# A hand-written schedule, re-dealt: side jobs, gate steps, denominators and queue order of a two-layer recurrent block on one core

## What is computed

```python
xn = layernorm(x)
# s: differential attention, 8 heads of 32 features, two maps per head with 16 features each
scores = einsum('bqhif,bkhif->ibhqk', q, k) * 16 ** -0.5
att = softmax(scores)[0] - 0.2 * softmax(scores)[1]
o = einsum('bhqk,bkhe->bqhe', att, v)
s = ((o * rsqrt(mean(o * o) + eps) * norm_w) @ Wo.T + bo) * (1 - 0.2)
# g: per token the two best of 8 experts, softmax of their two logits, low-rank product
gate = sum(one_hot(top2) * softmax(top2 values))
g = silu(2.0 * einsum('btr,bte,eor->bto', xn @ compress.T, gate, routed))
x = x + s * g
```

## Time and profile before

| what | value |
|---|---|
| median of three runs | 1316.97 us (1316.34, 1316.97, 1319.7) |
| the profiled execution | 1319.7 us, of which the span is 1317.9 us |
| layer 0 (to the last exponential) | up to about 650 us of the span |
| PE, PEld | 1215.7 us (92%), 755.9 us (57%) |
| DVE, ACT, POOL | 954.9 us (72%), 675.7 us (51%), 594.1 us (45%) |
| mean granted clock of TensorE | 0.969 |

### The profile page before, as it was taken

One profiled execution on the slowest core, in us unless ns is written; L12 is line 12 of the kernel. 1 busy time (PEld: TensorE's weight loads), 2 busy tenths in 40 slices (PEclk: granted clock), 3 DMA queues, 4 the chain that ended last, 5 costly groups with the idle time before them and its releaser, 6 DMA issues. The chain is left out here.

```text
span 1317.9 us, 27919 instructions
## 1 busy us (share of the span) xinstructions
PE 1215.7 (92%) x10768; PEld 755.9 (57%) x10768; DVE 954.9 (72%) x2088; ACT 675.7 (51%) x1297; POOL 594.1 (45%) x613
## 2 busy tenths in 40 slices
PE   5899999999999999998859999998989999898997
PEld 4433443444434444443347786877768777786875
DVE  5776787877778787866346859676786967768675
ACT  2455656666666666665624434444444434434442
POOL 2156586766768676766533222131321213223131
PEclk9598999999999999999969999999999999999999
DMA  6644354454535354470220010100101000010100
GB/s 193 137 88 99 87 122 97 106 137 88 132 72 122 86 116 98 106 191 26 63 86 2 2 49 2 49 3 1 49 2 48 3 26 25 2 49 2 32 3 17
DMA packets 57972, 86.36 MB, mean 66 GB/s; under 512 B 8304, under 2 KB 38256, under 8 KB 57840
## 3 DMA queue, kind: packets, MB, share of 16 engines
q1 hardware_dynamic: 57840, 84.58, 26.7%
HBM read 50.40 MB, written 33.55 MB: 64 GB/s over the span
## 5 line engine op out<-in xcount | busy, mean ns | idle before, releaser
L975 DVE TENSOR_REDUCE negmax<-s_bank 128x1 f32<-128x512 f32 x512 | 331.4, 678 | 53.3 <-PE s_bank L669 52.8
L1139 POOL TENSOR_TENSOR room<-room 128x512 f32<-128x512 f32 x248 | 309.2, 1279 | 105.5 <-ACT room L816 105.5
L816 ACT ACTIVATE room<-t_bank 128x512 f32<-128x512 f32 x512 | 286.6, 599 | 76.0 <-PE t_bank L679 73.9
L669 PE MATMUL s_bank<-kst,qst 48*128 48x512 f32 x512 | 217.0, 491 | 13.5 <-DVE negmax L975 9.2
L679 PE MATMUL t_bank<-qst,kst 50*128 50x512 f32 x512 | 200.3, 466 | 12.2 <-ACT room L816 9.9
L679 PEld LDWEIGHTS t_bank<-qst,kst 50*128 50x128 f32 x512 | 81.3, 188 | 126.4 <-ACT room L816 75.6
L1857 POOL TENSOR_TENSOR win<-rt,apart 128x512 f32<-128x512 f32 x32 | 42.0, 1332 | 231.5 <-DVE rt L1682 231.5
L692 PE MATMUL a_bank<-room,v 128*32 128x512 f32 x1024 | 139.0, 615 | 0.0
L1844 POOL TENSOR_TENSOR ex<-ex,rc 128x256 f32<-128x256 f32 x64 | 41.9, 655 | 189.0 <-DVE rc L1710 189.0
L1725 DVE STREAM_TRANSPOSE room<-ex 32x256 f32<-32x256 f32 x256 | 111.1, 434 | 10.1 <-POOL ex L1844 4.1
L669 PEld LDWEIGHTS s_bank<-kst,qst 48*128 48x128 f32 x512 | 86.1, 193 | 37.1 <-DVE negmax L975 29.6
(11 more groups left out here) (258 smaller groups left out, 2274.5 us busy)
## 6 DMA issues: line engine op xcount, KB each, us to landing
park<-qk_h SPq DMA_DIRECT2D x128, 128.0 KB, 2.4
qst<-park SPq DMA_DIRECT2D x64, 192.0 KB, 3.6
kst<-park SPq DMA_DIRECT2D x64, 192.0 KB, 4.3
park<-qk_l SPq DMA_DIRECT2D x64, 128.0 KB, 2.4
room<-in_x SPq DMA_DIRECT2D x8, 512.0 KB, 5.7
xr<-in_x SPq DMA_DIRECT2D x8, 512.0 KB, 6.2
room<-x SPq DMA_DIRECT2D x8, 512.0 KB, 4.2
out<-so SPq DMA_DIRECT2D x32, 128.0 KB, 1.7
```

The lines of the kernel that those rows point to most:

```text
L669: pe.matmul(s_bank[S_BANK[w]][:, :], qst[slot][rows, j, c * P:(c + 1) * P], kst[slot][rows, j, :], start=True, stop=True).then_inc(m.s_don ...
L816: act.activation(probs[:, c, j, :], t_bank[w % 2][:, :], ACT.Exp, scale=SCALE0).then_inc(m.exp_done, 1)
L975: dve.tensor_reduce(negmax[:, i_par, 2 * odd + j, c:c + 1], s_bank[S_BANK[w]][:, :], X, ALU.max, negate=True).then_inc(m.max_done, 1)
L1139: add = pool.tensor_tensor(sums[:, pair, h, :], probs[:, 2 * pair, h, :], probs[:, 2 * pair + 1, h, :], ALU.add)
```

## The change

The tables of the schedule are dealt anew, and two orders are edited. No operation is added or removed.

- Side jobs change steps (`SLOTS`, `JOBS`): the second XT goes before the first V of the quarter; PROJ of quarter 4 goes from (1, 9) to (1, 3); PROJ 5 from (2, 1) to (2, 3); TA 2 and 3 from (1, 3) and (1, 5) to (1, 5) and (1, 7); the M jobs from w = 7 to w = 9; WF 1 and 2 from (2, 9) and (2, 13) to (2, 11) and (2, 14); V 0 of the next batch goes before PROJ 7.
- Denominators go from w = 1 and 7 to w = 3 and 7, where each stands behind a value step; the value bank's copy from w = 8 to 9; the denominators' copy from (0, 11) to (0, 10).
- Gate steps, normalisation and squares change steps.
- In SyncE's order `place_max` of quarter 1 goes ahead of `load_x`, `load_residual` and the weights; `place_max` of quarters 2 and 3 goes behind a park and a fill each; the stores are spread.
- In GpSimd's order `add_parts` goes ahead of `add_maps`, the first residual behind `add_pair(2, 0)`, the second behind `rstd_of`.

```diff
-SLOTS = ((0, 1), (0, 3), (0, 5), (0, 7), (0, 9), (0, 13), (0, 15),
+SLOTS = ((0, 1), (0, 3), (0, 5), (0, 9), (0, 11), (0, 13), (0, 15),
          (1, 1), (1, 3), (1, 5), (1, 7), (1, 9), (1, 11), (1, 13), (1, 15),
-         (2, 1), (2, 5), (2, 7), (2, 9), (2, 13),
-         (3, 1), (3, 5), (3, 7), (3, 9), (3, 13), (3, 15))
-JOBS = (("XT", 1, 0), ("V", 0, 2), ("XT", 1, 1), ("M", 1, 1), ("V", 0, 3), ("TD", -1, 0), ("TA", -1, 0),
-        ("TA", -1, 1), ("TA", -1, 2), ("TA", -1, 3), ("M", 2, 0), ("PROJ", 4, 0), ("ZT", -1, 0), ("OT", -1, 0), ("OT", -1, 1),
+         (2, 3), (2, 5), (2, 9), (2, 11), (2, 14),
+         (3, 1), (3, 5), (3, 9), (3, 11), (3, 13), (3, 15))
+JOBS = (("XT", 1, 0), ("XT", 1, 1), ("V", 0, 2), ("M", 1, 1), ("V", 0, 3), ("TD", -1, 0), ("TA", -1, 0),
+        ("TA", -1, 1), ("PROJ", 4, 0), ("TA", -1, 2), ("TA", -1, 3), ("M", 2, 0), ("ZT", -1, 0), ("OT", -1, 0), ("OT", -1, 1),
         ("PROJ", 5, 0), ("WF", -1, 0), ("M", 3, 1), ("WF", -1, 1), ("WF", -1, 2),
-        ("PROJ", 6, 0), ("WF", -1, 3), ("M", 4, 0), ("PROJ", 7, 0), ("V", 1, 0), ("V", 1, 1))
+        ("PROJ", 6, 0), ("WF", -1, 3), ("M", 4, 0), ("V", 1, 0), ("PROJ", 7, 0), ("V", 1, 1))
...
-STATS, NORM_ENDS, NORMS = ((2, 11), (2, 12)), (2, 14), ((3, 10), (3, 11), (3, 12), (3, 14))
-GATE = ((1, 7), (1, 8), (1, 11), (1, 12), (1, 13), (1, 14), (1, 15), (2, 3), (2, 4), (2, 7), (2, 8), (2, 10),
-        (2, 15), (3, 0), (3, 2), (3, 3), (3, 4), (3, 6))
-GATE_EXP = (2, 13)
-SQUARES = ((1, 11), (1, 12), (1, 14), (2, 0))
-SUM_STEPS, EVAC_STEP, DEVAC = (1, 7), 8, (0, 11)
+STATS, NORM_ENDS, NORMS = ((2, 11), (2, 12)), (2, 13), ((3, 10), (3, 12), (3, 14), (3, 15))
+GATE = ((1, 5), (1, 6), (1, 7), (1, 13), (1, 14), (1, 15), (2, 5), (2, 6), (2, 7), (2, 13), (2, 14), (2, 15),
+        (3, 1), (3, 2), (3, 3), (3, 4), (3, 5), (3, 6))
+GATE_EXP = (3, 0)
+SQUARES = ((1, 11), (1, 12), (1, 13), (1, 14))
+SUM_STEPS, EVAC_STEP, DEVAC = (3, 7), 9, (0, 10)
```

SyncE's order in `body(b)`:

```diff
+                place_max(i + 1, 1)
                 if b < B - 2:
                     load_x(b + 2)
                 if b:
                     load_residual(b - 1)
                 if last:
                     shared.load_weights(sp, io1)
-                place_max(i + 1, 1)
-                place_max(i + 2, 2)
-                if not last:
-                    park_parts(i + 4)
-                    fill_stacks(i + 4, 0)
-                    park_parts(i + 5)
-                    fill_stacks(i + 5, 1)
-                place_max(i + 3, 3)
-                for t in range(2):
-                    if b:
-                        store_x1(b - 1, t)
+                for hf in (1, 2):
+                    if not last:
+                        park_parts(i + 3 + hf)
+                        fill_stacks(i + 3 + hf, hf - 1)
+                    place_max(i + hf + 1, hf + 1)
+                if b:
+                    store_x1(b - 1, 0)
                 if not last:
                     park_parts(i + 6)
                     fill_stacks(i + 6, 2)
                 if b:
+                    store_x1(b - 1, 1)
+                if not last:
+                    place_max(i + 4, 0)
+                if b:
                     store_x1(b - 1, 2)
```

GpSimd's order in `body(b)`:

```diff
                 add_pair(b, 0, 1)
+                if not last:
+                    add_parts(b + 1)
                 if not first:
                     add_maps(b - 1)
...
                 add_pair(b, 1, 1)
+                add_pair(b, 2, 0)
                 if not first:
                     residual(b - 1, 0)
-                add_pair(b, 2, 0)
-                if not first:
-                    residual(b - 1, 1)
-                if not last:
-                    add_parts(b + 1)
                 add_pair(b, 2, 1)
                 if b < B - 2:
                     rstd_of(b + 2)
                 if not first:
+                    residual(b - 1, 1)
                     residual(b - 1, 2)
```

More of the change, by code:

```diff
@@ L569, in body @@
                 if b:
+                    store_x1(b - 1, 1)
+                if not last:
+                    place_max(i + 4, 0)
+                if b:
                     store_x1(b - 1, 2)
                 if not last:
-                    place_max(i + 4, 0)
                     park_parts(i + 7)
```

## The result

The changed kernel takes 1334.63 us (median of four runs, 1329.73 to 1339.92), against 1317.55 us for the kernel before in runs beside it. The ratio is 1.0129, with a 95% interval of 1.0082 to 1.0176: slower by 1.3%. The forecast was 1323.0, its range ended at 1332, and slower was its likeliest sign. So the sign is right, and the size lies outside the range. The profiled execution of the changed kernel took 1343.76 us, with a span of 1341.8; its counterpart of before 1319.7 and 1317.9.

The account below looks back on a forecast made before the run. TensorE was taken to set the pace, busy 72.9 of 75.0 us a batch. Steady batches +7.2, batch 0 +3 and batch 7 -4 gave +6.2 us on the median 1316.97, so 1323, range 1308 to 1332.

Parts of the forecast that it names:

- likeliest sign: Whole kernel: slower by over 0.3% had chance 0.52, within 0.3% 0.25, faster 0.23.
- rule (a): After XT or PROJ, misc frees 1.50 us later; two bare steps leave 0.75 us idle, three times a batch: 2.25 us.
- bare steps (2, 1) and (2, 2): Start of quarter 2, left without denominators and PROJ: (2, 2) waits for the exponential of (2, 0), 0.7 us a batch.
- Gate step 7: At (2, 6) VectorE arrives after GpSimd's pair starts and waits 1.1 us; the tile of (2, 11) then waits 0.7.
- Batch 0: First batch: stack wait and slow clock go (-7.8 us); two 2.5 us waits for maxima's rows, slow clock 6: +3.
- batch 7: Last batch: wait for maxima behind weights, its slow clock and a wait for GpSimd's sums go: -4 us.
- Net: 2.4 + 1.4 + 0.7 + 1.3 - 4.6 = +1.2 us a batch, x 6 = +7.2: Steady batches 1 to 6: job waits, M alone, bare steps and quarter 2, less VectorE's backlog and small savings.
- much slower: Rival: maxima's rows come after TensorE at every (2, 0), clock perhaps falling; +14 us, 1337; chance 0.12.
- M alone at w = 9: Steps 8 to 10: fourth tile held by exponentials, 0.38 us a quarter, 0.25 in quarter 1; 1.4 a batch.
- VectorE's backlog: Steady batch: excess at (3, 1), (3, 5), (1, 7) and other steps goes or is replaced, 3.5 us a batch.
- faster: Rival: in batch 0 place_max rows of quarters 2 and 3 pass the fill and land in time; 1307; chance 0.23.
- no change: Rival: VectorE comes first at (2, 6), or batch 0's waits don't slow the clock; 1317 to 1319; chance 0.25.

Follow-up runs that it names:

- experiment 3: Changed kernel with only gate steps 6 to 8 moved earlier, to (2, 3), (2, 4) and (2, 5): 1329.84 us, ratio 1.0080 to the kernel before.
- experiment 5: Changed kernel run again with nothing edited: 1339.67 us, ratio 1.0151 to the kernel before.
- experiment 6: Changed kernel with place_max of quarters 2 and 3 ahead of the fill, still behind the park: 1331.42 us, ratio 1.0092 to the kernel before.
- experiment 2: Changed kernel with only PROJ 5 moved back from (2, 3) to (2, 1): 1322.72 us, ratio 1.0028 to the kernel before.
- experiment 10: Changed kernel with the denominators back at w = 1 and 7: 1335.28 us, ratio 1.0127 to the kernel before.
- experiment 1: Changed kernel with four jobs re-dealt: V (0, 3), XT (0, 5), PROJ 4 (1, 1), TA 1 (1, 3), PROJ 5 (2, 1): 1315.41 us, ratio 0.9967.
- experiment 7: Kernel before with only the denominators moved, from w = 1 and 7 to 3 and 7: 1308.56 us, ratio 0.9924.

## Why the prediction was right and wrong

**Right: the mechanisms.** Each of the three job waits stands where it was put, 0.74 to 0.75 us, six times, by rule (a). The bare steps (2, 1) and (2, 2) cost 0.71 (said 0.7). Gate step 7 met GpSimd and took 1.17 us (said 1.1), and its whole term, removed in experiment 3, is 0.56 of the 0.7 given to the wait at (2, 11). Quarter 3 is 1.8 shorter (said 1.5). Batch 0 has the two waits behind the fill and the slow clock behind them, batch 7 has neither of its waits. The differences by quarter at full clock are +0.95, +1.24, +1.60 and -1.80; said were +0.5, +0.55, +1.45 and -1.5.

On gate step 7 the prediction could not settle who comes first; the trace does. GpSimd started at 337.36, VectorE at 337.52, 0.16 us later, for 1.17 us; in experiment 3, ahead of GpSimd, the same operation takes 0.18. By "SBUF — State Buffer", section "SBUF: two separate sides", of the Trainium skill, whichever of the two starts first holds the shared port pair for its whole instruction. The trace agrees: the later starter waited out the add.

**The step that failed** is "Net: 2.4 + 1.4 + 0.7 + 1.3 - 4.6 = +1.2 us a batch, x 6 = +7.2", and it failed twice.

First, it has no term for the granted clock. I priced the steady batch at 1.00 throughout, because the earlier trace rows show 1.00 in each quarter and I took both falls of before for the work of single waits of 1.64 and 1.87 us. In the changed kernel no wait in a steady batch exceeds 0.75 us, and the clock still fell at (2, 11), for 1.63 us each time: 8.2 us in the profiled execution, 3.3 and 4.9 in experiments 5 and 6. The trace of before already spoke against my reading. The stretch of 18.1 us at 0.63 in the earlier trace rows, which I put behind the wait of 1.64 us, is three in the main: 3.3 us at half clock behind the wait, 3.4 us at full clock, and 10.2 us at half clock behind two waits for exponentials of 0.44 and 0.56 us.

```profile
95.40:98.70 3.30, 3.30 (x19) 0.59 (x16) 1.38 (x3) 0.60 (x1) 1.92 (x2) 0.50 0.68 158
98.70:102.10 3.40, 2.40 (x21) 0.82 (x17) 2.34 (x4) 2.42 (x5) 3.40 (x4) 1.00 0.52 111
102.10:112.30 10.20, 9.94 (x40) 2.84 (x39) 7.96 (x20) 3.95 (x8) 6.88 (x5) 0.50 0.38 69
...
100.54 0.49 PE L679 MATMUL t_bank<-qst,kst 50*128 50x512 f32 x1 [0.44 <-ACT room L816]
...
101.61 0.50 PE L679 MATMUL t_bank<-qst,kst 50*128 50x512 f32 x1 [0.56 <-ACT room L816]
```

The rival "much slower" did have a falling clock, but tied to rows of maxima that come late at (2, 0); the rows were in time in every steady batch, and the clock fell without them. Removing the idle of (2, 1) to (2, 5) (experiment 2) or the gate's wait (experiment 3) ended the falls in quarter 2 in the profiled executions of both. That supports the idle of this quarter as their cause, but these are single profiles, falls moved to quarter 1 in experiment 2, and in experiment 10, where (2, 1) and (2, 2) are covered and the wait at (2, 5) is not, quarter 2 of batch 3 still lost clock.

Second, the terms at full clock were undersized by 0.8 in batches 1 to 5. By the timeline, M alone at w = 9 costs 2.1 us a batch, not 1.4 (0.62, 0.54, 0.37 and 0.54 by quarter, each step against the shortest of equal content), just past its bound of 2.0: steps 9 to 11 of quarter 0 take 0.83 + 0.49 + 2.71 us. What I left out is that the value matmuls of w = 11 also need the value bank, whose copy now sits at w = 9; their weight load waits 0.3 to 0.4 us for it. No run moved M alone; the nearest check is quarter 0 of experiments 1 and 7, which differ there in M, the V behind it and two copies on ScalarE: 17.36 against 16.86, 0.5 of the 0.62. And VectorE's backlog at (1, 7), counted as gone, stayed: 0.31 us there. In batch 6 the cost is 3.1, because that batch of before, 73.91 us, had less backlog to lose, and I took all six as alike. The bounds were added up wrongly as well: those of the four terms less 4.6 come to -2.8 and +3.7 a batch, and the text has -1.0 and +3.0.

By the profiled executions, then, said +6.2, measured +24.0. The missing 17.8 us are: clock in batches 2 to 6, 8.2; steady terms, 5.9 (13.1 less 7.2); batch 0, 1.9; batch 7, 1.5; unassigned, 0.3. The medians differ by 17.1 us, 10.9 more than said, and 9.3 of that would be the steady terms and the two outer batches, if they are alike in every execution. So the falls are the largest item of the longest execution. What they leave room for at the median, 1.6 us, is one fall; how many it had is not on record.

**Batch 0** was +4.9 instead of +3. The two waits were of 1.1 us each on TensorE (2.0 for its weight loads), not 2.5, and the 6.8 us at half clock behind each cost half of their busy time, 3.3 us, where I took 3. What I left out is the rest: the stretch of 3.4 us at 82 us, 1.7 us by the same estimate, and the job waits and bare steps of a steady batch, which stand in batch 0 too. Experiment 6, without any wait for rows, still has a batch 0 of 74.0 us, where before less the 7.8 us of its wait and clock would have 68.6. That experiment gets 7.2 us back against the first profile and 9.0 against experiment 5, whose batch 0 also began with more slow clock; experiment 1 gets 9.5 back with the jobs alone. One move in the queue is also what the rival "faster" needed: two small rows not behind the fill.

**Batch 7** was -2.5 instead of -4; its wait for the rows and the one for GpSimd's sums both went. I had counted the bare steps' loss of about 0.5 us once. Experiment 10 shows what the move of the denominators costs there: 2.3 us, 0.6 to 0.9 in three of the four quarters, which is more than the 1.5 missing.

**The rival "no change"** rested on VectorE coming first at (2, 6). Experiment 3 makes that so, and the kernel is still 0.8% slower: the job waits outweigh the 4 us that it turned on.

**What stays open** is what decides in which batch the clock first falls. In experiment 6 batches 1 to 3 kept it and 4 to 6 lost it at the same instructions and the same waits, and in experiment 5 it was 1 to 4 and 5 to 6. The runs of the changed kernel spread from 1329.7 to 1343.8 us; five falls at 1.64 would be 8 of these 14 us. The execution with the least time has a mean clock of 0.971 and the longest 0.963, but one of 1337.7 us has 0.970, so the clock does not order them all.

## What to carry to other kernels

Where many side jobs share one bank, lay a long TensorE step between a job with a two-stage drain (1.50 us here) and the next job; two bare steps (0.75 us) leave the rest idle. A re-dealt schedule is a bundle: try its edits one by one, since here one alone gave 0.8% and the bundle lost 1.3%. Before you put a slow stretch down to one long wait, cut it finer: in the earlier trace rows most of it stood behind two short ones. And on an engine that is 93% busy, give each new idle stretch a second price, that of the slower clock behind it, and look in each queue for small transfers that many wait for standing behind large ones that nobody needs yet.

## What the runs showed of the hardware

The granted clock fell to half in a stream in which PE was busy 73.5 of 78.6 us and no single wait exceeded 0.75 us; in batch 0 of before it fell behind the wait of 1.64 us, went back up 3.4 us later, then fell again behind 0.44 and 0.56 us and stayed down for 10.2 us. A longer single wait did not settle it either: in batch 0 of the changed kernel 1.13 and 1.10 us of idle were followed by a fall, and at the second of these places 1.25 us (experiment 3) and 1.18 us (experiment 10) were not. At the same instructions and waits it fell in some batches and not in others. The price at (2, 11) was 1.6 us each time. Two rows of 8 KB behind a fill in one queue held TensorE's weight loads for 2.0 us and its matmuls for 1.1, twice, and cost nothing ahead of it. A VectorE operation of 0.18 us took 1.17 us when a GpSimd add had started 0.16 us before it.
